# Comparisons of a 2:4 sparsity mask with one operand in PSUM, and one product bank fewer

## The reference

```
x = x + 0.5 * ffn(layernorm(x))      # "G"
x = x + mamba(layernorm(x))          # "M"
x = x + 0.5 * ffn(layernorm(x))      # "F"
ffn:   h = silu(x @ w_gate) * (x @ w_up)            # 2048 wide
       of each 4 neighbours of h, only the 2 largest in magnitude are kept
       out = h_sparse @ w_down
mamba: u = silu(conv4(xn @ W_in.T)); delta = softplus(u @ Wd1.T @ Wd2.T + bd2)
       state = exp(delta * A) * state + delta * u * B_t     # 1024 channels x 16 states
       y = sum over states of C_t * state, + u * W_D, gated by silu(xn @ W_skip.T), @ W_out.T
```

## Time and profile before

| | |
|---|---|
| time, median of 3 runs | 3793.55 us (3790.35 to 3793.97) |
| the profiled execution | 3794.77 us, span 3793.0 us |
| TensorE, VectorE, ScalarE, GpSimd busy | 3429.7, 3166.7, 1942.6, 2602.7 us |
| mean granted clock of TensorE | 0.958 of 2.4 GHz |
| first scan, end of the last | 327.7 us, 3588.8 us |

### The profile page before, as it was taken

How to read it: one execution, slowest core, us unless ns; L and a number is a source line. 1 busy time by engine, 2 the same in 40 slices (tenths; PEclk the granted TensorE clock), 3 DMA queues, 4 the chain that set the end, 5 groups by cost and what they waited for, 6 DMA issues and landing times. The chain is left out here.

```text
span 3793.0 us, 39493 instructions
## 1 busy us (share of the span) xinstructions
PE 3429.7 (90%) x11823; PEld 2115.7 (56%) x11888; DVE 3166.7 (83%) x3560; ACT 1942.6 (51%) x2587; POOL 2602.7 (69%) x2069
## 2 busy tenths in 40 slices
PE   7999989999999999999989998888888899888689
PEld 5665556556655565556555664556444565455355
DVE  3545898788989899998998899998999999999822
ACT  4324656556455664656454665465455565444220
POOL 0005776666867779777787788778988888789700
PEclk9999999999999999999999999999999899999899
DMA  8556466656646576456654665547545556455332
GB/s 329 211 169 192 144 200 214 203 164 213 209 164 211 172 230 197 153 194 215 211 166 157 209 214 187 183 142 228 182 153 171 168 194 205 145 166 175 99 107 99
DMA packets 247571, 696.50 MB, mean 184 GB/s; under 512 B 27632, under 2 KB 27888, under 8 KB 237680
## 3 DMA queue, kind: packets, MB, share of 16 engines
q1 hardware_dynamic: 173632, 559.72, 42.6%
q10 hardware_dynamic: 73728, 134.25, 13.7%
HBM read 619.94 MB, written 76.55 MB: 184 GB/s over the span
## 5 line engine op out<-in xcount | busy, mean ns | idle before, releaser
L1197 POOL TENSOR_TENSOR db<-du,Bb 128x512 f32<-128x512 f32 x1024 | 1332.8, 1302 | 885.3 <-DVE decay L1074 551.4
L1208 POOL TENSOR_TENSOR y<-y,pr 128x512 f32<-128x512 f32 x1024 | 1356.0, 1324 | 101.3 <-DVE pr L1084 101.1
L1074 DVE TENSOR_TENSOR_SCAN decay<-decay,db 128x512 f32<-128x512 f32 x1024 | 1251.7, 1222 | 133.4 <-ACT decay L769 121.8
L769 ACT ACTIVATE decay<-delta,aneg 128x512 f32<-128x512 f32 x1024 | 700.6, 689 | 1183.1 <-DVE pr L1084 1180.3
L584 PE MATMUL main<-zhi,wunit 128*128 128x512 f32 x2048 | 932.8, 455 | 29.4 <-DVE zlo L1006 26.1
L647 PE MATMUL side<-h,wdown 128*128 128x512 f32 x2048 | 931.2, 599 | 23.6 <-ACT sq L851 8.9
L585 PE MATMUL main<-zlo,wunit 128*128 128x512 f32 x2048 | 820.9, 401 | 0.0
L586 PE MATMUL main<-zhi,wunit 128*128 128x512 f32 x2048 | 819.9, 400 | 0.0
L1084 DVE TENSOR_TENSOR pr<-decay,Cb 128x512 f32<-128x512 f32 x1024 | 702.5, 686 | 29.7 <-issue 0.9
L647 PEld LDWEIGHTS side<-h,wdown 128*128 128x128 f32 x2048 | 388.9, 191 | 453.3 <-issue 405.2
L584 PEld LDWEIGHTS main<-zhi,wunit 128*128 128x128 f32 x2048 | 394.7, 193 | 203.1 <-issue 100.6
(11 more groups left out here) (87 smaller groups left out, 2674.2 us busy)
## 6 DMA issues: line engine op xcount, KB each, us to landing
wunit<-hl_dram SPq DMA_DIRECT2D x480, 512.0 KB, 4.1
wdown<-down_w_dram SPq DMA_DIRECT2D x256, 256.0 KB, 3.2
wmam<-mam_dram SPq DMA_DIRECT2D x128, 512.0 KB, 4.2
Bb<-bc_dram ACTq DMA_DIRECT2D x256, 256.0 KB, 4.2
Cb<-bc_dram ACTq DMA_DIRECT2D x256, 256.0 KB, 5.2
hl_dram<-wunit SPq DMA_DIRECT2D x32, 512.0 KB, 3.1
skip_dram<-skb SPq DMA_DIRECT2D x64, 256.0 KB, 3.9
delta<-skip_dram SPq DMA_DIRECT2D x16, 1024.0 KB, 6.2
```

What stands on the lines that cost most here:

```text
L769: nc.scalar.activation(decay[u % BANKS][:], delta[:, e, :], ACT.Exp, scale=aneg[:, e, n:n + 1]).then_inc(sem["decay_ready"], 1)
L1074: nc.vector.tensor_tensor_scan(decay[u % BANKS][:], decay[u % BANKS][:], db[u % RING][:], 0.0, ALU.mult, ALU.add).then_inc(sem["state_read ...
L1197: nc.gpsimd.tensor_tensor(db[u % RING][:], du[:, e, :], Bb[m % ROWS][:], ALU.mult).then_inc(sem["input_ready"], 1)
L1208: nc.gpsimd.tensor_tensor(y[:, e, :], y[:, e, :], pr[u % RING][:], ALU.add).then_inc(sem["sum_ready"], 1)
```

## The change

Each comparison is made as soon as its newest member is there. Member j of a quad (j = 1, 2, 3) is compared with the members before it, in one instruction that is 512 j wide, two ticks after its up product, at the end of VectorE's tick. The newest magnitude is read from a PSUM bank `mag` that ScalarE writes, spread over the members; the older ones are read from `ab` in SBUF, which now has three members. So ScalarE writes members 1 and 2 twice (to `mag` and to `ab`), 0 only to `ab`, 3 only to `mag`. The Abs of a member waits until the comparison before it is done, since there is one bank. The list of matmuls in `wins` follows the new order of the comparisons.

The bank comes from the products: `MAINS` goes from 3 to 2. The two Silus move ahead of the Exps of the first quarter. `load_rows` follows `BANKS` by name, with the same value. `PAUSES` has 46 ticks in place of 43, `STARTS` is moved by up to five ticks, and the planner's costs are changed. The number of comparisons (192) and their elements are the same.

```diff
--- before.py
+++ after.py
...
 EXP_LEAD = 1
-MAINS = 3
+MAINS = 2
 SIDES = 3
...
 WIN_TICKS, DOWN_TICKS = (3, 3, 4, 4), (6, 7, 8, 9)
-PAUSES = {0: 9, 47: 8, 480: 26}
+PAUSES = {0: 9, 34: 1, 43: 1, 47: 7, 224: 3, 448: 1, 480: 24}
 LAST_TICKS = 12
...
 
-STARTS = (68, 130, 193, 249, 305, 359, 404, 449, 508)
+STARTS = (67, 131, 191, 253, 310, 363, 407, 454, 511)
 
...
         tensor = {"dt": 6.9, "bc": 1.8, "fold": 0.9, "msum": 0.9, "mean": 0.9, "vsum": 0.9, "var": 0.9, "dl": 0.9, "win": 0.7}
-        unit = 1.86
+        unit = 1.94
 
...
                 cost += 0.7
-            cost += 4.5 * (tick - 2 in self.base)
-            cost += 3 * (tick in self.ffn_start or tick in self.split_x_at) + 3 * (tick in self.scale_at) + 3.5 * (tick in self.gate_at)
+            cost += 3.5 * (tick - 2 in self.base)
+            cost += 2.5 * (tick in self.ffn_start or tick in self.split_x_at) + 3.0 * (tick in self.scale_at) + 2.5 * (tick in self.gate_at)
             return cost + 3 * (tick in self.du_at)
...
         h = [sb(f"h{k}", [P, 4, L]) for k in range(2)]
-        ab = sb("ab", [P, 4, L])
+        ab = sb("ab", [P, 3, L])
         cmp = sb("cmp", [P, 6, L], bf16)
...
         side = [pb(f"side{k}") for k in range(SIDES)]
+        mag = pb("mag")
         decay = [pb(f"decay{k}") for k in range(BANKS)]
...
             "product_ready", "side_ready", "gate_read", "up_read", "part_ready",
-            "magnitude_ready", "quad_compared",
+            "magnitude_ready", "compared",
             "squares_ready", "quarter_ready", "root_ready", "scaled", "high_part_ready", "normed_ready",
...
                 if j == 0:
-                    pe.wait_ge(sem["quad_compared"], s + 1)
-                for k, (c, sign) in enumerate((((0, 0), (1, 0), (2, 0)), ((0, 1), (3, 0), (4, 0)),
-                                               ((1, 0), (3, 0), (5, 1)), ((2, 0), (4, 0), (5, 0)))[j]):
+                    pe.wait_ge(sem["compared"], 3 * s + 3)
+                for k, (c, sign) in enumerate((((0, 0), (1, 0), (3, 0)), ((0, 1), (2, 0), (4, 0)),
+                                               ((1, 0), (2, 0), (5, 1)), ((3, 0), (4, 0), (5, 0)))[j]):
                     mm = nc.tensor.matmul(bank[:], signs[:, sign, :], cmp[:, c, :], start=(k == 0), stop=(k == 2))
...
                 nc.scalar.activation(decay[u % BANKS][:], delta[:, e, :], ACT.Exp, scale=aneg[:, e, n:n + 1]).then_inc(sem["decay_ready"], 1)
-                if u % HE == 1:
+                if u % HE == BANKS - 1:
                     load_rows(u // HE + 2)
...
             def magnitude(pair):
+
                 s, j = divmod(pair, 4)
                 act.wait_ge(sem["up_read"], pair + 1)
-                if j == 0 and s:
-                    act.wait_ge(sem["quad_compared"], s)
-                nc.scalar.activation(ab[:, j, :], h[s % 2][:, j, :], ACT.Abs).then_inc(sem["magnitude_ready"], 1)
+                if s or j > 1:
+                    act.wait_ge(sem["compared"], 3 * s + max(0, j - 1))
+                if j:
+                    nc.scalar.activation(mag[:], h[s % 2][:, j, :], ACT.Abs).then_inc(sem["magnitude_ready"], 1)
+                if j < 3:
+                    ins = nc.scalar.activation(ab[:, j, :], h[s % 2][:, j, :], ACT.Abs)
+                    if j == 0:
+                        ins.then_inc(sem["magnitude_ready"], 1)
 
...
                         copy_quarters(key)
+                if done is not None and done % 4 == 1:
+                    silu(pair_of(done) - 1)
+                    silu(pair_of(done))
                 upto(share(units, 0, 4).stop)
...
                     x_high(plan.split_x_at[tick])
-                if done is not None and done % 4 == 1:
-                    silu(pair_of(done) - 1)
-                    silu(pair_of(done))
                 if n is not None and n + AHEAD < FFN:
...
 
-            def compare_with(s, i):
-                m, first = 3 - i, (0, 3, 5)[i]
-                if i == 0:
-                    dve.wait_ge(sem["magnitude_ready"], 4 * s + 4)
-                    if s:
-                        wait_job(dve, ("win", s - 1, 3))
-                ins = nc.vector.tensor_tensor(cmp[:, first:first + m, :], ab[:, i:i + 1, :].broadcast_to([P, m, L]),
-                                              ab[:, i + 1:4, :], ALU.is_ge)
-                if i == 2:
-                    ins.then_inc(sem["quad_compared"], 1)
+            def compare(pair):
+
+                s, j = divmod(pair, 4)
+                first = j * (j - 1) // 2
+                dve.wait_ge(sem["magnitude_ready"], pair + 1)
+                if j == 1 and s:
+                    wait_job(dve, ("win", s - 1, 3))
+                nc.vector.tensor_tensor(cmp[:, first:first + j, :], ab[:, 0:j, :], mag[:].unsqueeze(1).broadcast_to([P, j, L]),
+                                        ALU.is_ge).then_inc(sem["compared"], 1)
 
...
                 jobs = plan.jobs_at[tick - 1] if tick else []
-                last = tick - 2 == plan.base[-1]
-                if last:
-                    for i in range(3):
-                        compare_with(len(plan.base) - 1, i)
+                before = plan.product_at[tick - 2] if tick > 1 else None
+                compared = pair_of(before) if before is not None and is_up(before) and pair_of(before) % 4 else None
+                if compared == PRODUCTS // 2 - 1:
+                    compare(compared)
                 begin(share(units, 0, 4))
...
                         shifted_tap(key, 0)
-                if tick - 2 in plan.base and not last:
-                    compare_with(plan.base.index(tick - 2), 0)
-                    compare_with(plan.base.index(tick - 2), 1)
                 for key in jobs:
...
                         shifted_tap(key, 2)
-                if tick - 2 in plan.base and not last:
-                    compare_with(plan.base.index(tick - 2), 2)
+                if compared is not None and compared < PRODUCTS // 2 - 1:
+                    compare(compared)
                 finish(share(units, 3, 4))
```

## The result

The changed kernel takes 3693.2 us (median of four runs, 3688.2 to 3697.1) against 3793.8: ratio 0.9735, 95% interval 0.9718 to 0.9752, 100 us faster. The forecast was 3740 (3695 to 3800). The direction holds, and so does the mechanism of the gain; the size is almost double what the sum gave, and the time lies just outside the range, beside rival B (3690 us).

The account below looks back on a forecast made before the run. VectorE was taken to set the pace from 1425 to 3589 us, TensorE from 328 to 1425 us. Terms -105 + 5 + 20 + 30 - 5 = -55 us took 3794.8 to 3740 us, range 3695 to 3800.

Parts of the forecast that it names:

- rival B: VectorE's relief passes through whole, the Silu move and two banks cost nothing: 3690 us, or some 3680; chance 0.12.
- Part 1: VectorE's comparisons with one operand in PSUM escape contention with GpSimd, 3.63 us per quad: -105 us.
- The +5 us for GpSimd: GpSimd runs with less in hand behind a faster VectorE, causing single waits: +5 us (0 to 20).
- Parts 2 and 3: ScalarE: two more Abs per quad and Silus ahead of first-quarter Exps make VectorE's Exps late: +20 us (0 to 60).
- Part 4: Two product banks: TensorE's products wait for Silus and multiplications that read the banks: +30 us (0 to 223).
- An eighth of 223: Share taken as real of TensorE's 223 us lateness at the two product banks: +30 us.
- Part 5: Placement: first scan one tick earlier, mostly paid back; changed costs counted as nothing: -5 us (-10 to 0).
- Rival A: The two banks decide: TensorE and ScalarE tied in one tick, more lateness real, slower, 3843 us; chance 0.18.
- Rival C: No relief: magnitude bank slow or GpSimd the bound, gain halved, within 0.2%, 3793 us; chance 0.08.
- The signs: Comparisons under 2 us, TensorE's comparison wait under 30 us, new `h` waits, longer VectorE Exp wait, shorter GpSimd scan wait.
- what was to prove the forecast wrong towards slower: Prediction wrong if new bank waits exceed 100 us and VectorE's waits for TensorE rise with them.

Follow-up runs that it names:

- experiment 3: Kernel before with two product banks, Silus first, and the comparisons' second operand read from a PSUM bank filled with ones: 3711.1 us, ratio 0.979.
- experiment 1: Kernel before with only the two Silus moved ahead of the first-quarter Exps, three product banks kept: 3792.0 us, ratio 1.0002.
- y_sbuf: Changed kernel with the newest magnitude `mag` in SBUF in place of a PSUM bank: 3840.7 us, ratio 1.0124.
- y_sbuf3: Changed kernel with `mag` in SBUF and three product banks: 3805.7 us, ratio 1.0036.
- experiment 7: Changed kernel with the two Silus put back behind the first-quarter Exps, two banks kept: 3777.7 us, ratio 0.9966.
- experiment 4: Kernel before with the new order of comparisons and its two more Abs per quad, `mag` in SBUF, three banks, old Silus and placement: 3816.6 us, ratio 1.0061.
- experiment 5: The runs y_sbuf and y_sbuf3: changed kernel with `mag` in SBUF, 3840.7 us, and with three product banks as well, 3805.7 us.
- experiment 2: Kernel before with the two Silus ahead of the first-quarter Exps and two product banks in place of three: 3814.2 us, ratio 1.0055.

## Why the prediction was wrong

Start from before and take the runs in turn: Silus first +1, two banks +20, PSUM operand -100, new order -4, placement -17; together -100. These are differences along one chain of runs, so they must add up to the measured change; what they tell is the split, in this order, each to 6 to 9 us.

- **Part 1, the PSUM operand: right in its sum, in part by luck.** -105 was forecast and -100 measured, with the forms within 1% of the durations taken from the centring. The split was wrong. All of 95 us was counted where VectorE sets the pace, and a third of 24 where TensorE leads; experiment 3 shows about three quarters in both (76 of 100, 18 of 23). One error takes off what the other adds. The relief was also a little larger than the sum had it, since 3.63 us adds up single comparisons and the 5.84 are of three that overlap: against 3.49 it is 54 x 2.35 = 127 us and not 119. The +5 us for GpSimd wasn't there: VectorE waits 11 us for it before and after.
- **Parts 2 and 3, ScalarE: the first step that failed.** +20 us for the Silus and the second Abs; measured +1 for the Silus and -4 for the order with its Abs, 23 us less. The lateness of the second unit's Exp was weighed too high, the earliness of the third one's too low; VectorE's wait for Exps grows by 5 us in experiment 1. It is 142 us in the changed kernel; what that growth costs there no run isolates.
- **Part 4, two banks: right in kind, its size not settled.** +30, measured +20 with the old comparisons and 33 in `y_sbuf` against `y_sbuf3`. In the changed kernel itself it can't be measured, since three product banks, three `side`, two `decay` and `mag` would be nine banks, and there are eight. The lateness is real: TensorE waits 111 us for bank readings in the changed kernel (93 for the Silu, 18 for the multiplication). But it mostly takes the place of other waits of TensorE, that for comparisons above all. "An eighth of 223" was a guess; what could have been set against it is the 127 us wait for comparisons, of which the trace of before shows 104.
- **Part 5, placement: the second step that failed.** -5, measured -17 (and +6 in the kernel before). The cost table was put at nothing; taking it back costs 9 us, taking back pauses and starts 10. It takes no work out, but it says where the units go.
- **The sum.** 23 + 10 + 12 + 5 us too high, less 5 for part 1: 45 us. All charges erred on one side by these runs; the 10 for the banks is hardly clear of noise. Rival B, relief whole, gave nearly the time that came, but not for its reason: the banks do cost, not all of the relief passes through, and the placement paid for it. That the time lies beside B is luck. Rival A doesn't occur in the change; its mechanism does in experiment 7, with the Silus in their old place. Rival C fell with the forms.
- **The signs** named ahead came: comparisons under 2 us, TensorE's wait for them under 30, new rows for `h`, a longer wait for Exps, and a shorter one of GpSimd for the scan (551 us before, 469 after). So did what was to prove the forecast wrong towards slower: bank waits above 100 us (111), and VectorE's five longest waits for TensorE grew from 323 to 346 us. The kernel was faster all the same, so that test was badly set: 23 us more of waiting stand beside 135 us less of work.

That contention with GpSimd is the cause of the gain is shown by experiments 3, 4 and 5 and the shortest and longest durations: the operand's place alone makes the difference, with the comparisons unblocked before the first scan either way. That the placement helps only beside the new comparisons was measured; why was not traced.

## What to carry to other kernels

Compare the mean duration of an instruction with its shortest, and look at what GpSimd does under the long ones: 350 us of comparisons held 127 us in which VectorE only stood, and one operand moved to PSUM ended it. A wait that a change adds is not a cost until the waits that it replaces are taken off; count an engine's waits as one sum, and look for the cost at the engine that sets the pace (experiment 2: 98 us of new waits, 5 us more in TensorE's sum, 22 us more in VectorE's, 20 us of time). When a ring gets tighter, the order in which an engine serves it can come to matter (nothing in the kernel before, 88 us in the changed one), so such edits are to be judged together.

## What was not expected of the hardware

- A blocked VectorE instruction lets not one but many GpSimd instructions pass: six in the earlier trace rows and six under the longest comparison of experiment 2 (9.7 us in place of 1.75), until GpSimd itself has to wait. Once in, the instructions that follow it directly are hardly touched (1300 and 714 ns against 3602 for the first).
- An Abs from SBUF takes 592 ns into PSUM and 618 into SBUF (192 of each in the changed kernel). For Abs, what the Trainium skill says (ScalarE: Activation LUTs, Step-by-step: what each stage is for), that ScalarE writes to PSUM faster than to SBUF, agrees with the trace. In the prediction I took the Exp's 689 and 631 ns for the reverse, but those two are unlike: the Exp into PSUM has a scale per partition (`aneg`), the other has none. In the kernel before a Ln with a bias per partition, from PSUM into SBUF, takes as long as the first, which suggests that this operand makes the difference and not the destination:

```profile
L851 ACT ACTIVATE sq<-side,eps 128x512 f32<-128x512 f32 x24 | 16.5, 688 | 2.1 <-PE side L626 1.8
```
